# Transposing both halves of a finished row behind the second product chunk instead of one half behind each of two chunks

## What is computed

```
adj_hat = adj + eye;  dis = 1 / sqrt(sum(adj_hat, axis=1))
x = layernorm(x + relu((adj_hat * dis[:, None] * dis[None, :]) @ (x @ W) + b))
s = x @ weight
o = pair_norm(relu(s + adj @ s + x @ self_weight))   # one mean and one scale over all nodes
x = layernorm(x + o)
```

## Time and profile before

| | |
|---|---|
| Median of 3 runs | 1850.84 us (1850.59 to 1851.46) |
| The profiled execution | 1850.69 us; its span 1848.8 us, 1.9 us less |
| Busy, share of the span | PE 89%, DVE 78%, PEld 68%, ACT 65%, POOL 1% |
| Chain that ended last, by engine | PE 63%, DVE 16%, DMA 15%, ACT 4%, issue 2% |
| Mean granted TensorE clock | 0.957 of full speed |

### The profile page before, as it was taken

How to read it: one execution, slowest core, us unless ns; L and a number is a source line. 1 busy time by engine, 2 the same in 40 slices (tenths; PEclk the granted TensorE clock), 3 DMA queues, 4 the chain that set the end, 5 groups by cost and what they waited for, 6 DMA issues and landing times.

```text
span 1848.8 us, 20668 instructions
## 1 busy us (share of the span) xinstructions
PE 1652.1 (89%) x7682; PEld 1262.7 (68%) x7682; DVE 1450.5 (78%) x1893; ACT 1203.4 (65%) x1636; POOL 21.2 (1%) x42
## 2 busy tenths in 40 slices
PE   1088898989998999899999999999989999999993
PEld 1055564656665677677778888888868888877872
DVE  4477687797988989877767765755599999999997
ACT  3486696777776666545555545544568888888875
POOL 0000000000000000100000000000000000000001
PEclk7589999999999999999999999999999999999995
DMA  9999999999999974934454545545589999999943
GB/s 397 422 422 421 420 422 421 420 421 417 421 399 391 377 289 174 342 140 178 159 182 161 184 179 191 189 169 203 207 325 386 386 386 386 385 379 367 387 181 91
DMA packets 87460, 572.04 MB, mean 309 GB/s; under 512 B 8960, under 2 KB 17152, under 8 KB 19264
## 3 DMA queue, kind: packets, MB, share of 16 engines
q1 hardware_dynamic: 84928, 562.07, 77.4%
q0 software_dynamic: 2432, 8.65, 1.3%
HBM read 566.49 MB, written 4.19 MB: 309 GB/s over the span
## 4 chain that ended last, share of the span: by engine, by line
PE 63%; DVE 16%; DMA 15%; ACT 4%; issue 2%; SPq 0%; ACTq 0%; POOLq 0%; DVEq 0%
PE acc L1044 17%; PE acc L1046 16%; PE acc L1050 16%; DVE raw_low L736 6%; DMA s<-in_adjN 5%; DMA raw<-in_adjT 4%; DMA o<-in_adjT 3%; DMA s<-in_adjT 3%; PE pC L1025 2%; ACT hi L558 2%; DVE s L756 1%; DVE zr_low L736 1%; DVE s L742 1%; DVE o_low L736 1%; DVE ux L802 1%
## 5 line engine op out<-in xcount | busy, mean ns | idle before, releaser
L1044 PE MATMUL acc<-hi,rhi 128*128 128x512 f32 x1792 | 728.7, 407 | 76.3 <-DVE raw_low L736 63.2
L736 DVE TENSOR_TENSOR raw_low<-raw,hi 128x1024 fp32r<-128x1024 f32 x530 | 629.5, 1222 | 48.4 <-ACT hi L558 43.6
L558 ACT ACTIVATE hi<-raw 128x1024 fp32r<-128x1024 f32 x530 | 545.3, 1054 | 108.8 <-PE acc L1050 55.3
L1046 PE MATMUL acc<-raw_low,rhi 128*128 128x512 f32 x1536 | 607.9, 396 | 0.0
L1050 PE MATMUL acc<-hi,rlo 128*128 128x512 f32 x1792 | 558.4, 393 | 0.0
L1044 PEld LDWEIGHTS acc<-hi,rhi 128*128 128x128 f32 x1792 | 340.9, 190 | 219.6 <-DVE raw_low L736 115.1
L1050 PEld LDWEIGHTS acc<-hi,rlo 128*128 128x128 f32 x1792 | 340.4, 190 | 74.2
L1046 PEld LDWEIGHTS acc<-raw_low,rhi 128*128 128x128 f32 x1536 | 293.4, 191 | 60.8 <-issue 3.1
L735 DVE TENSOR_TENSOR rlo<-zr,rhi 128x256 fp32r<-128x256 f32 x123 | 52.1, 424 | 170.4 <-ACT hi L558 170.4
L558 ACT ACTIVATE hi<-zr 128x1024 fp32r<-128x1024 f32 x146 | 152.8, 1059 | 39.5 <-PE acc L1050 22.5
L552 ACT ACTIVATE rhi<-zr 128x256 fp32r<-128x256 f32 x123 | 50.8, 413 | 193.5 <-PE acc L1050 193.5
(11 more groups left out here) (200 smaller groups left out, 1726.1 us busy)
## 6 DMA issues: line engine op xcount, KB each, us to landing
raw<-in_adjT SPq DMA_DIRECT2D x265, 1024.0 KB, 5.0
zr<-in_adjT SPq DMA_DIRECT2D x73, 1024.0 KB, 5.8
o<-in_adjT SPq DMA_DIRECT2D x42, 1024.0 KB, 16.4
s<-in_adjT SPq DMA_DIRECT2D x40, 1024.0 KB, 16.6
o<-in_adjN SPq DMA_DIRECT2D x38, 1024.0 KB, 22.5
raw<-in_adjN SPq DMA_DIRECT2D x33, 1024.0 KB, 15.8
s<-in_adjN SPq DMA_DIRECT2D x26, 1024.0 KB, 20.9
zr<-in_adjN SPq DMA_DIRECT2D x15, 1024.0 KB, 22.6
```

Of the source, the lines that this page charges most:

```text
L558: S.activation(hi[n % DEEP][:, :], slice_of(chunk, j), ACT.Copy).then_inc(hi_ready, 1)
L736: V.tensor_sub(low_of(chunk, j), slice_of(chunk, j), hi[n % DEEP][:, :].bitcast(f32)).then_inc(slice_split, 1)
L1044: T.matmul(banks[h][:, :], a, hi[n % DEEP][:, part], start=opens, stop=False, skip_group_check=True)
L1046: T.matmul(banks[h][:, :], a, low_of(chunk, j)[:, part], start=False, stop=False, skip_group_check=True)
```

## The change

On TensorE, both halves of a finished row are transposed behind chunk 1; before, half 0 was transposed behind chunk 0 and half 1 behind chunk 1. No other engine's list changes, and no instruction is added or removed.

```diff
                 row, at = since_row(n)
                 if row is None:
                     return
-                if at == 0:
-                    turn_sum(row, 0)
                 if at == 1:
-                    turn_sum(row, 1)
+                    for h in range(H):
+                        turn_sum(row, h)
                 if at == 3:
                     turn_x1(row, 0)
```

## The result

| | before | after |
|---|---|---|
| Median | 1850.59 us (1849.00 to 1851.74, 7 runs) | 1857.20 us (1854.83 to 1858.39, 7 runs) |
| Ratio after to before | | 1.0034, 95% interval 1.0023 to 1.0046 |
| The profiled execution | 1850.69 us, span 1848.8 | 1856.17 us, span 1854.4 |
| Chain that ended last, PE and DVE | 63%, 16% | 61%, 18% |

The changed kernel is 6.6 us slower by the medians; the interval of the ratio allows 4.3 to 8.5. The two profiled executions are 5.5 us apart. Forecast were 5.7 us, 1856.5 us.

The account below looks back on a forecast made before the run. TensorE was taken to set the pace while rows are finished; six rows each losing 0.82 us of stall plus 0.13 us, 0.95 together, gave 5.7 us and a median of 1856.5 us, range 1853.8 to 1858.4.

Parts of the forecast that it names:

- VectorE did not wait before and waits now: At L834 in six rows: half 0 comes late, so VectorE starts 1.17 us late, idle about 1.1 us.
- The cover of the split of chunk 3: Between split and TensorE's chunk 3: only 0.41 us of cover, so chunk 3 starts 0.82 us late.
- A short stall costs 0.13 us besides its length: In chunk 3: a chunk behind a short stall runs 5.57 us against 5.44, making 0.95 us a row.
- The transposes as such cost nothing: On TensorE behind chunk 1: grouping the eight transposes is worth 0.05 us of its time a row.
- Rows 7 and 0 are covered: Both cost nothing: row 7's wait for x swallows the delay; row 0's half 0 arrives 0.11 us early.
- One of its bounds: Upper bound, six rows: a release 0.2 us slower, or a longer first matmul, gives 1.25 a row, 7.5 us.
- The middle of the forecast: Six rows (6 to 1) at 0.95 us each, 5.7 us slower, median 1856.5 us.
- The delay is not given back later: Denies the rival that later row-sum waits shrink, giving back at most 4.4 us: 1852.0 us; chance 8%.
- The wait that never binds: Rival at L834: half 0 arrives in time, only the grouping's 0.05 us each stays: 1850.4 us; chance 5%.
- The clock did not fall behind the new stalls: Denies the rival that dual chunks behind new stalls take 7.17 us, not 5.57: 15.3 us, 1866 us; chance 5%.

Follow-up runs that it names:

- e10: Changed kernel with the group of eight transposes put ahead of chunk 1's last four matmuls; 1852.17 us, 1.0001 of the kernel before.
- e9: Changed kernel with the group of eight transposes put ahead of chunk 1's last two matmuls; 1855.61 us, 1.0020 of the kernel before.
- e3: Changed kernel with VectorE's update of half 0 waiting for both halves' transposes; 1860.83 us, 1.0051 of the kernel before.
- e4: Changed kernel with the group of both halves behind chunk 1's first slice instead of its second; 1850.73 us, 0.9997 of the kernel before.
- e5: Changed kernel with the group of both halves behind chunk 0 instead of chunk 1; 1850.88 us, 0.9998 of the kernel before.
- e2: Kernel before with half 0 moved behind chunk 1 for rows 7 and 0 only; 1852.34 us, 1.0005 of the kernel before.
- e6: Kernel before with VectorE's row sum between its two splits of chunk 0, rows 6 to 1; 1846.25 us, 0.9969 of the kernel before.
- e1: Kernel before with half 0 moved behind chunk 1 for rows 6 to 1 only; 1858.31 us, 1.0041 of the kernel before.
- e7: Changed kernel with VectorE's row sum between its two splits of chunk 0, rows 6 to 1; 1852.11 us, 1.0001 of the kernel before.
- e8: Kernel before with the row sum between chunk 0's splits and both halves grouped behind chunk 1's first slice; 1843.97 us, 0.9965 of the kernel before.

## Why the prediction was right

**VectorE did not wait before and waits now.** Forecast was a start of L834 1.17 us late with about 1.1 us of idle time in six rows; in row 5 it is 1.15 us late and idle for 1.08, with six waits, 6.5 us in all.

**The cover of the split of chunk 3 is 0.41 us in the trace, 0.35 after the release.** This is the step on which the sum stands. Chunk 3 was to start 0.82 us late and starts 0.79 late. Four doses show the cover as a straight line with a foot (waits of row 5, and a fifth of the five rows):

| L834 waits | 0.17 (e10) | 0.63 (e9) | 1.08 (changed) | 1.52 (e3) |
|---|---|---|---|---|
| TensorE idle before chunk 3 | none | 0.25 | 0.73 | 1.15 |
| cost of a row, us | 0.04 | 0.51 | 0.94 | 1.40 |
| worked out in advance | -0.05 | 0.50 | 0.95 | 1.38 |

**A short stall costs 0.13 us besides its length.** Chunk 3 took 5.58 us behind the new stall, 0.14 more than before; behind 0.25 us in e9 it took 5.58 as well, behind 1.15 in e3 5.62. Without this term the forecast would have been 0.8 us lower. At the foot of the line the expectation left the term out, and e10 pays 0.09 of it without a stall.

**The transposes as such cost nothing.** Place, not grouping: e4 and e5.

**Rows 7 and 0 are covered.** e2 for both; in row 0 with 0.1 us to spare, as worked out. In e3, where the wait overruns that cover, row 0's L834 starts 9.28 us after its row sum (1343.66 to 1352.94) and not 8.95 (1332.17 to 1341.12), 0.33 later, as worked out.

**Not luck.** The terms came out one by one, so the forecast was not right by errors that cancel. One of its bounds is put wrongly: a release 0.2 us slower and a first matmul 0.08 us longer make about 1.25 a row (1.23) only together, and the prediction says "or". The middle of the forecast does not rest on it.

**The rivals.** The delay is not given back later: the waits for L826 stayed at 7.6 us, and e3 and e6 show both signs passing through in full. The wait that never binds fell with the first row read. The clock did not fall behind the new stalls: it stayed at 0.99 from 786 to 1338 us. Since idle times of equal length can be followed by either level (last section), one kernel would be thin evidence; but rows 5 to 1 of the changed kernel, e1, e3, e7 and e9 have 25 such stalls, of 0.24 to 1.16 us, and every chunk 3 behind them took 5.57 to 5.63 us, none near 7.17. The Trainium skill, page "TensorE: Matmul & The Clock Gate", section "A second HAM failure mode: psum-queue depth-cycling", describes a kernel in which frequent small idle times make the clock fall and rise. These traces do not show it at these lengths, six times in 550 us.

**What stays open.** The medians are 6.6 us apart, the profiled executions 5.5, and the prediction had 5.7. What the medians have more is inside the interval. One profile a kernel cannot say whether the late half also makes the slow chunk of the next section more frequent.

## What to carry to other kernels

An operation whose result is due soon should be placed by its reader's time, not by its own cost: the group of eight transposes took 0.8 us of TensorE's time inside chunk 1 (e4) as behind it, but behind it they let VectorE wait, and with it all that is queued behind the wait, by more than the 0.35 us of slack that its next split has. Before moving a step, read how long its reader stands or runs ahead of the result, and how much cover the next thing in that reader's list has; here 1.17 minus 0.35 us, and 0.13 for the broken run, times six was the answer, to within the measurement. And where one engine sets the pace, the same reading names the gain: the stalls of TensorE for the row sum were in the table of waits all along, and moving the sum ahead by one split gave 5.6 us (3.7 to 8.0 by the interval).

## What the runs showed that was not expected

The spread of single runs, 3.6 us among seven of the changed kernel, has a part that one can see around rows 7 and 6: the clock after an idle time of 1.9 to 3.2 us differs between profiles. In row 7 TensorE waits 1.63 to 1.93 us for ScalarE's L606 ahead of the transposes into pC. Here is the stretch from these transposes, of half 1, to the products that make its second-layer input, in the changed kernel (wait 1.63) and then in e3 (wait 1.93) (stretch, its us, PE, PEld, DVE, ACT, POOL busy, clock, DMA share, GB/s):

```profile
776.62:779.87 3.25, 3.25 (x17) 2.76 (x17) 3.25 (x4) 2.33 (x3) 0.00 (x0) 1.00 1.00 364
```

```profile
778.12:782.96 4.84, 4.84 (x16) 3.96 (x17) 3.68 (x4) 2.32 (x3) 0.00 (x0) 0.65 1.01 405
```

At a granted clock of 1.00, the upper of the two levels (2.4 GHz), it takes 3.25 us; at 0.65, for the most part at the lower (1.2 GHz), it takes 4.84: 1.6 us, as much as the chunk in the earlier trace rows lost. The clock in e3 was not still low from the stall of 6.33 us at the start of the row: it was 0.50 right behind that stall and 0.98 from 768 to 776 us. Nor does the length of the wait alone decide: in e1 it is also 1.93 us, and the same stretch takes 3.24.

Chunk 0 behind row 6 shows the same. In e7 and in e8, which have the same idle time of 2.05 us before it, it reads:

```profile
787.42:794.59 7.17, 7.17 (x24) 5.72 (x25) 3.93 (x5) 0.52 (x1) 0.00 (x0) 0.76 0.31 126
```

```profile
786.60:792.16 5.56, 5.56 (x24) 4.58 (x25) 3.93 (x5) 0.52 (x1) 0.00 (x0) 1.00 0.40 161
```

Behind the longer 3.19 us of the kernel before it was 7.17 us, and behind 3.22 us in e5 it was 5.56. So an idle time of this size can cost 1.6 us more or not, and its length alone does not tell which. That one and the same kernel falls on either side from run to run would fit the spread, but with one profile a kernel it is not shown. From row 7's sum to row 6's the profiled executions take 39.5 us (before) and 39.6 (changed) but 41.9 in e3 and e9 and 41.8 in e5. So a difference of one or two microseconds between two single runs of these kernels says nothing, and the stretch of five rows, which repeats to 0.2 us in kernels with the same waits (494.13 and 494.32; 489.44 twice), was the better measure.
